# Layer 1 attention of a two-layer cross-attention kernel: probabilities turned by DMA transposes instead of TensorE transposes

## The reference, cut to what matters

```
Q = (X @ Wq.T + bq).reshape(b, 56, 16, 64)
KV = (encoder_out @ Wkv.T + bkv).reshape(b, 1500, 16, 128)
K, V = (KV[..., :64], KV[..., 64:])
scores = einsum('bqhd,bkhd->bhqk', Q, K) / 8
weights = softmax(scores, axis=-1)
attn = einsum('bhqk,bkhd->bqhd', weights, V).reshape(b, 56, 1024)
out = attn @ Wo.T + bo
```

## Time and profile before

| what | value |
|---|---|
| median of 3 runs | 1374.76 us |
| the profiled execution's own time | 1373.72 us |
| its span in the trace | 1372.0 us |
| mean granted TensorE clock | 0.973 |
| TensorE busy | 1226.6 us, 89% of the span |
| VectorE busy | 1025.5 us, 75% |
| ScalarE busy | 769.0 us, 56% |
| GpSimd busy | 395.4 us, 29% |

### The profile page before, as it was taken

The page is one execution under the profiler, slowest core; times in us unless marked ns, Lnnn a source line. Parts: engine busy times, 40 slices in busy tenths (PEclk is TensorE's granted clock), DMA queues, the critical chain, the costliest instruction groups (busy, mean ns, idle before and its releaser), DMA issues.

```text
span 1372.0 us, 27813 instructions
## 1 busy us (share of the span) xinstructions
PE 1226.6 (89%) x10406; PEld 772.9 (56%) x10408; DVE 1025.5 (75%) x1661; ACT 769.0 (56%) x1013; POOL 395.4 (29%) x248
## 2 busy tenths in 40 slices
PE   0868999999999997888799999999999999999974
PEld 0335566666666566334456666656666666666642
DVE  6657666666666646877788888888888888888877
ACT  0534455555555455455666666666666666666642
POOL 5357665666666414332000000000000000000000
PEclk9989999999999997999999999999999999999996
DMA  5333344344234420010011110011110011110000
GB/s 150 78 79 86 85 106 108 80 112 110 79 97 108 113 61 7 0 46 0 3 43 46 46 39 25 27 45 45 45 44 19 27 45 45 45 44 24 1 0 14
DMA packets 29717, 74.66 MB, mean 54 GB/s; under 512 B 6384, under 2 KB 14960, under 8 KB 29664
## 3 DMA queue, kind: packets, MB, share of 16 engines
q1 hardware_dynamic: 23408, 70.78, 17.6%
q10 hardware_dynamic: 6256, 3.16, 0.9%
HBM read 42.30 MB, written 0.46 MB: 31 GB/s over the span
## 4 chain that ended last, share of the span: by engine, by line
PE 69%; DVE 13%; issue 8%; ACT 6%; ACTq 3%; DVEq 0%; POOL 0%
PE bank L825 13%; PE bank L807 13%; PE bank L767 8%; PE bank L683 7%; PE bank L707 5%; PE bank L711 5%; PE bank L724 4%; DVE bank_max L1495 3%; ACTq L415 2%; DVE region L1636 2%; ACT region L1139 2%; PE bank L796 2%; PE bank L848 2%; PE bank L785 2%; DVE e_row L1456 2%
## 5 line engine op out<-in xcount | busy, mean ns | idle before, releaser
L1456 DVE CUSTOM_DVE_ANT_0 e_row<-bank,region 112x1500 f32<-112x1500 f32 x128 | 220.2, 1720 | 128.9 <-PE bank L683 128.8
L1174 ACT CAST region<-bank 125x768 f16<-125x768 f32 x224 | 178.7, 798 | 207.9 <-PE bank L767 207.9
L1139 ACT ACTIVATE region<-bank 125x896 f32<-125x896 f32 x192 | 176.0, 917 | 210.4 <-PE bank L711 210.4
L807 PE MATMUL bank<-region 128*128 128x500 f16 x1008 | 236.1, 380 | 14.7 <-ACT e_row L1165 13.3
L1514 DVE TENSOR_TENSOR region<-bank,region 125x768 f16<-125x768 f32 x224 | 209.6, 953 | 25.7 <-ACT region L1174 25.7
L1495 DVE TENSOR_REDUCE bank_max<-bank 128x1 f32<-128x500 f32 x336 | 208.9, 671 | 11.9 <-PE bank L807 11.9
L513 POOL TENSOR_TENSOR region<-c_in,region 125x1536 f16<-125x1536 f32 x16 | 49.7, 3108 | 562.2 <-ACT region L1189 562.2
L767 PEld LDWEIGHTS bank<-ident,e_row 128*125 128x125 f32 x1344 | 175.9, 188 | 31.3 <-DVE region L1514 5.5
L767 PE MATMUL bank<-ident,e_row 128*125 128x128 f32 x1344 | 179.6, 274 | 3.3 <-DVE region L1514 2.6
L1165 ACT ACTIVATE e_row<-bank,neg_max 128x1500 f32<-128x1500 f32 x112 | 169.7, 1515 | 20.1 <-DVE neg_max L1499 19.9
L807 PEld LDWEIGHTS bank<-region 128*128 (+1 forms) x1008 | 93.7, 98 | 116.4 <-issue 12.8
(11 more groups left out here) (211 smaller groups left out, 1483.4 us busy)
## 6 DMA issues: line engine op xcount, KB each, us to landing
c_in<-in_ctx SPq DMA_DIRECT2D x32, 750.0 KB
region<-region SPq DMA_DIRECT2D x64, 192.0 KB, 2.7
region<-in_mask_Bx1xSxS_if SPq DMA_DIRECT2D x32, 328.1 KB
region<-region SPq DMA_DIRECT2D x64, 96.0 KB, 2.5
region<-region SPq DMA_DIRECT2D x8, 750.0 KB
g_w<-region SPq DMA_DIRECT2D x8, 750.0 KB
g_w<-in_L_ffn_rt_gate ACTq DMA_DIRECT2D x1, 1024.0 KB, 9.8
u_w<-in_L_ffn_rt_up ACTq DMA_DIRECT2D x1, 1024.0 KB, 17.8
```

Source lines behind the costliest of these rows:

```text
L807: last = pe.matmul(bank[:, k, 0:4 * KP], q1[:, ql, b, 128 * t:128 * (t + 1)], c_t1[par][:, cl, 4 * k:4 * k + 4, 0:KP], start=(ql == 0 and ...
L1139: act.activation(p0[:, 2 * i:2 * i + 2, :], ring0("s", h, i)[0:KP, :, 0:HALF_ROWS], ACT.Exp, scale=SCALE0)\
L1174: act.copy(p_high1[grp][:, UC * u:UC * (u + 1), 128 * at:128 * (at + 1)], pair_chunks(unit_no(1, par, ("turn", t, u)), 128)).then_inc(sem( ...
L1456: dve.tensor_tensor_reduce(out=masked.rearrange("p (a k) -> p a k", a=3), in0=bank[0:R0, 0:3, 0:4 * KP], in1=mask_bias[par][:].rearrange(" ...
```

## The change

Layer 1's loop is written anew.

- The scores have two sets of three banks, 0 to 2 and 3 to 5, in turn (`score_banks1`), and one semaphore step for each tile. Scores of tile n wait for the exponential of tile n-2.
- One VectorE instruction takes the maximum of 1500 columns in place of four.
- `e_row` is not scaled any more. VectorE scales the row's sum and takes its reciprocal (`dve_inv1`); ScalarE writes the high half straight from `e_row` with that factor (`act_high1`, one instruction of 1500 columns), VectorE the low half (`dve_low1`, one instruction of 1500). Both go to `halves1`, two buffers of 128 x 2 halves x 12 chunks x 128 columns (padded from 125), which lie in memory that holds weights earlier.
- One DMA transpose for each tile, on SyncE's queue, turns both halves into `p1` (`sync_turn1`): 24 blocks of 128x128 float16, 786,432 bytes. The high half of tile n waits until tile n-2 has been turned, since they share a buffer.
- The context's halves are turned by such a DMA as well (`sync_turn_context1`), issued behind tile 1's; TensorE's `pe_prep` and ScalarE's copies remain for batch 0 alone.
- SyncE's queue has in every batch: the load of the next context, the turns of tiles 0 and 1, the context's turn, tiles 2 to 4, the copy to `c_keep1`, tiles 5 and 6. The engine waits before each for what it needs, in this order.
- The products move back: group 0's three parts come after tile 6's scores slot and in the next batch's slots 0 and 1; group 1's in its slots 3 to 5. Each group has a bank of its own, 6 and 7.

The diff's core, with what the prediction speaks of:

```diff
+        U_BANK1 = (6, 7)
+        def score_banks1(par, t):
+            first = 3 * ((t + par) % 2)
+            return bank[:, first:first + 3, 0:4 * KP]
...
+        def turned1(b, par, t):
+            return sem(f"turned1_{(t + par) % 2}"), 56 * (b - par) + 16 * ((T1 * par + t) // 2 + 1)
+        def sync_turn1(sp, b, par, t):
+            grp = 0 if t < GROUPS1[1][0] else 1
+            first = GROUPS1[grp][0]
+            if t == first:
+                wait_apart(sp, "sp", (sem("pv_done1"), 2 * (b - 1) + grp + 1))
+            wait_apart(sp, "sp", (sem("low_done1"), b * T1 + t + 1))
+            sp.dma_start_transpose(p1[grp][:, :, :, 128 * (t - first):128 * (t - first + 1)].rearrange("p n c r -> p (n c) r"),
+                                   halves1[(t + par) % 2].rearrange("p n c k -> p (n c k)"))\
+                .then_inc(turned1(b, par, t)[0], 16)
+        def sync_turn_context1(sp, b, par):
+            wait_apart(sp, "sp", (sem("split_done1"), b + 1))
+            wait_apart(sp, "sp", (sem("scores1"), (b - 1) * T1))
+            sp.dma_start_transpose(c_t1[par].rearrange("p n c k -> p (n c) k"), c_split1.rearrange("p n c e -> p (n c e)"))\
+                .then_inc(sem("c_turned1"), 16)
...
             def layer1(b, par, first, last):
                 if not last:
                     sync_load_context(sp, 1, b + 1, 1 - par)
-                    sync_keep(sp, b + 1, 1 - par)
+                for t in range(T1):
+                    sync_turn1(sp, b, par, t)
+                    if t == 1 and not last:
+                        sync_turn_context1(sp, b + 1, 1 - par)
+                    if t == GROUPS1[1][0] and not last:
+                        sync_keep(sp, b + 1, 1 - par)
...
         def pe_scores1(pe, b, par, t):
...
-            wait(pe, sem("exp_done1"), b * T1 + t)
+            wait(pe, sem("exp_done1"), b * T1 + t - 1)
...
         def pe_pv1(pe, b, par, grp, first, end):
...
-                pe.wait_ge(sem("low_done1"), b * (2 * T1) + 2 * z)
-                wait(pe, sem("u_done1"), b * 2 + grp)
+                for t in (z - 2, z - 1):
+                    pe.wait_ge(*turned1(b, par, t))
+                wait(pe, sem("u_done1"), 2 * b + grp - 1)
...
-                    pe_turn(pe, 1, b, par, t, (0,))
-                    if t == 0:
-                        pe_turn(pe, 1, b, par, t, (1,))
-                    if t < 3 and not first:
-                        pe_pv1(pe, b - 1, 1 - par, 1, 4 * t, 4 * t + 4)
-                    if t >= 4:
-                        pe_pv1(pe, b, par, 0, 4 * (t - 4), 4 * (t - 3))
+                    if t < 2 and not first:
+                        pe_pv1(pe, b - 1, 1 - par, 0, 4 * (t + 1), 4 * (t + 2))
+                    if 3 <= t < 6 and not first:
+                        pe_pv1(pe, b - 1, 1 - par, 1, 4 * (t - 3), 4 * (t - 2))
+                    if t == 6:
+                        pe_pv1(pe, b, par, 0, 0, 4)
+                    if t == 6 and par == 0 and not first:
                         pe_proj1(pe, b)
...
         def act_exp1(act, b, par, t):
             act.wait_ge(sem("max_done1"), b * T1 + t + 1)
-            wait(act, sem("turned1"), (b * T1 + t - 1) * 2)
+            wait(act, sem("low_done1"), b * T1 + t - 1)
...
+        def act_high1(act, b, par, t):
+            act.wait_ge(sem("inv_done1"), 2 * (b * T1 + t) + 2)
+            if not (isinstance(b, int) and b == 0 and t < 2):
+                ready, count = turned1(b, par, t)
+                act.wait_ge(ready, count - 16)
+            act.activation(halves1[(t + par) % 2][:, 0, :, 0:KP], e_row[(t + par) % 2][:].rearrange("p (c k) -> p c k", c=KC),
+                           ACT.Copy, scale=row_inv[:, t:t + 1]).then_inc(sem("high_done1"), 1)
...
         def act_split1(act, b, par):
             act.wait_ge(sem(f"ctx_in1_{par}"), per_use(b, par, 16))
-            wait(act, sem("ct_turned1"), 2 * b)
-            wait(act, sem("kept1"), 16 * b)
-            act.copy(c_split1[0:KP, :, 0, :], c_in[par][:]).then_inc(sem("high1"), 1)
+            if not (isinstance(b, int) and b == 0):
+                act.wait_ge(sem("ct_turned1"), 2)
+                wait(act, sem("c_turned1"), 16 * (b - 1))
+                act.wait_ge(sem("kept1"), 16 * b)
+            act.copy(c_split1[0:KP, 0], c_in[par][:]).then_inc(sem("high1"), 1)
...
                     if t == 1 and not last:
                         act_split1(act, b + 1, 1 - par)
...
+                    act_high1(act, b, par, t)
                     if t < T1 - 1:
                         act_exp1(act, b, par, t + 1)
                     elif not last:
                         act_exp1(act, b + 1, 1 - par, 0)
...
         def dve_max1(dve, b, par, t):
-            for k in range(3):
-                dve.wait_ge(sem("scores1"), (b * T1 + t) * 3 + k + 1)
-                dve.tensor_reduce(bank_max[:, t, k:k + 1], bank[:, k, 0:4 * KP], AX.X, ALU.max, negate=True)\
-                    .then_inc(sem("bank_max"), 1)
...
+            dve.tensor_reduce(neg_max[:, t:t + 1], score_banks1(par, t), AX.XY, ALU.max, negate=True)\
+                .then_inc(sem("max_done1"), 1)
...
+        def dve_low1(dve, b, par, t):
+            dve.wait_ge(sem("high_done1"), b * T1 + t + 1)
+            half = halves1[(t + par) % 2]
+            dve.scalar_tensor_tensor(half[:, 1, :, 0:KP], e_row[(t + par) % 2][:].rearrange("p (c k) -> p c k", c=KC),
+                                     row_inv[:, t:t + 1], half[:, 0, :, 0:KP], ALU.mult, ALU.subtract)\
+                .then_inc(sem("low_done1"), 1)
...
             def layer1(b, par, first, last):
                 for t in range(T1):
                     nxt = (b, par, t + 1) if t < T1 - 1 else (b + 1, 1 - par, 0)
+                    dve_inv1(dve, b, par, t)
+                    if not (last and t == T1 - 1):
+                        dve_max1(dve, *nxt)
+                    dve_low1(dve, b, par, t)
...
```

204 lines of the change are left out of this document (61 added, 143 removed).

## The result

The kernel after takes 1506.95 us (median of 4, 1505.90 to 1507.38), the kernel before beside it 1374.74 (median of 4). The ratio is 1.0968, 95% interval 1.0943 to 1.0993: slower by 132 us. I had forecast slower, by 41. The time lies in the range and the sign is right; the size is off by a factor of three. The profiled execution took 1506.82 us, span 1505.1, mean granted clock 0.883 (before: 0.973).

The account below looks back on a forecast made before the run. The prediction took SyncE's queue of turns, copy and load to bound the changed loop at 44.3 us a batch, 3.2 more than now. 14 x 3.2 - 7 + 3 = +41 us on 1373.7 gave 1415, range 1285 to 1570.

Parts of the forecast that it names:

- D: Time for which one turn of 786,432 bytes holds the DMA engines, taken as 3.2 us, near the 16-engine copies' row.
- step 1: After the context's load lands: ScalarE's split 1.48, tile 1's high half 1.45 and low half 1.72, together 4.7 us.
- the formula: One batch's loop through SyncE's queue and ScalarE, four steps plus 0.5 for semaphores: 25.1 + 6D, 44.3 us.
- Both ends that I leaned on, 1.8 and 3.4: Estimates of a turn's time: 1.8 us from five engines' rate scaled to sixteen, 3.4 from 16-engine copies within the chip.
- rival C: Turns dearer than copies, 6.2 us each from 24 blocks going one by one; some 1670 us; chance 0.16.
- C's sign: What would show C: landings over 8 us with DMA engines busy throughout, or SyncE held for microseconds by an issue.
- step 2: Issue and landing 1.85 us plus three turns in line (tile 1's, the context's, tile 2's): 1.85 + 3D.
- step 3: Tile 4's high and low half, after tile 2's turn frees their buffer: 3.2 us.
- step 4: Tile 4's turn, the copy, turns of 5 and 6, the next load, before the next split: 14.85 + 3D.
- -7 + 3: Ends: batches 0 and 15 at 37.5 us each, -7 in all; last exponential to last copy-out about 18 us, +3.
- A: Turns as fast as five engines' ports suggest, D about 2.1: 1329 us, 1357 at worst with halved clock; chance 0.27.
- B: Queue does not hold turns behind the 5-engine transfers; 36 us a batch, 1298 us; chance 0.14.

Follow-up runs that it names:

- e1: Kernel after, with the context's copy moving 128 rows and the load cut in 112 and 13 rows: 1403.82 us, ratio 1.0208.
- e4: Kernel after, with only the high halves turned, 12 blocks a tile instead of 24 (output not the reference's): 1351.73 us, ratio 0.9834.
- e7: Kernel after, each tile's turn replaced by a plain copy of 128 pieces of 6144 bytes, nothing turned: 1391.92 us, ratio 1.0126.
- e5: Kernel after, copy and loads issued from ScalarE's queue, still on 5 engines, the load a batch earlier: 1417.06 us, ratio 1.0305.
- e3: Kernel after, each tile's turn replaced by a plain copy of the same 3072 pieces of 256 bytes, unturned: 1510.16 us, ratio 1.0986.
- e10: Kernel after, with GpSimd's subtraction waiting for tile 1's low half: 1481.46 us, ratio 1.0776.
- e9: Kernel after, copy and loads on ScalarE's queue and spread over 16 engines, loads a batch earlier, context's turn behind tile 1's: 1373.35 us, ratio 0.9990.
- e12: On e11, each tile turned by two DMAs, one per half, the high half's sent as soon as it is written: 1304.65 us, ratio 0.9492.
- e13: Kernel after with only the edit of two turns of 12 blocks a tile, copy and load unchanged: 1435.90 us, ratio 1.0447.
- e11: e9 and e10 together, against the kernel before: 1373.14 us, ratio 0.9985.

## Why the prediction was right and wrong

**That a line of transfers decides, and makes the kernel slower: right.** TensorE busy 68% and waiting for exponentials, ScalarE waiting for the load and for the turns of the buffers, all as forecast. e1 shows the five engines' part, e4 and e7 that the price of a turn is the other part. The sentence that the order of SyncE's queue is what holds a turn was too narrow: e5 took the two transfers out of that queue and the turns still took 7.6 to 10.3 us.

**"I take 3.2: near the 16-engine row": this step failed.** D is 3.9: 3.6 of transfer at 217 GB/s and 0.3 until the next. 6 x 0.7 = 4.2 us a batch, 59 of the missing 91 us; step 1 below is 22, and what is left, about 10, is the formula's own error (0.4 a batch), the batch before (41.0 and not 41.1) and the ends. Both ends that I leaned on, 1.8 and 3.4, came from copies in longer pieces. The lower one is what e7 shows for pieces of 6144 bytes, 430 GB/s. The rate of the earlier trace rows, which I followed, came out close to the turn's by luck: those copies move 3072 bytes in each of their 64 rows, and nothing in them said what pieces of 256 bytes cost (what held them at 215 to 234 GB/s no run shows). The price of 256-byte pieces was in no row, and I gave them 0.16 as rival C, which put it far too high at 6.2. C's sign came half true: the issue does hold SyncE. But e3 shows that this by itself costs nothing here: with copies of the same rate that are issued in 0.63 the kernel takes the same time.

**Step 1, 4.7 us: measured 6.3.** The high half is 1.55, and the low half beside GpSimd's subtraction 3.27. I named the subtraction as running beside and costed it at nothing. e10 prices this: 1.6 a batch, 25 us in all. This is a second step that failed, an overlap taken as free.

**Steps 2 to 4.** In the batch above, step 2 from 1091.02 to 1104.61 is 13.6 us (forecast with D = 3.9: 13.55); step 3 3.5 (3.2); step 4 from 1108.07 to the next split at 1134.90 26.8 (26.55). So the formula held for the kernel after: 25.1 + 6 x 3.9 + 1.6 = 50.1, measured 50.5 in the mean and 50.2 in this batch. On other kernels it is rougher. For e4, whose trace has half turns issued 1.7 us apart where nothing holds them (1051.86, then 1053.58), it gives 25.1 + 5 x 1.7 + 3.9 + 1.6 = 39.1, measured 40.3. For e7, with 1.8 for each of the five long copies and 3.9 for the context's turn, it gives 39.6, measured 42.9; it comes closer, 42.4, only if a copy is counted as its landing less the forecast's overhead, 4.2 - 1.85 = 2.35.

**Batch 0, batch 15 and the end.** Forecast -7 + 3. The loop alone makes +133 of +132 us, so both together are about -1. The end, in the timeline of the kernel after:

```profile
1453.29 0.19 ACT L1132 ACTIVATION_READ_ACCUMULATOR e_row<-bank,neg_max 128x1 f32 x1
...
1465.61 6.01 PE L798 MATMUL bank<-region,g_w 125*128 125x384 f16 x36
...
1471.66 0.49 ACT L1148 ACTIVATE region<-bank 128x384 f32<-128x384 f32 x1 [4.44 <-PE bank L798]
```

From the last read-out to the last copy-out are 18.4 us (forecast 18, before 15). The +3 holds, and the -7 was too much by some 3.

**Rivals.** A and B fall: in the kernel after no turn lands under 5.4 us, and no turn behind the copy lands before it has freed the engines. The clock that I priced only in A is real here as well, since TensorE idles 8.9 us before tile 2's scores and runs them at 0.50, 1.85 us longer. No run isolates what this costs in all; in the batch above the next wait, for a turn, mostly covers it.

**What I did not price: the two buffers.** The formula has them in it as waits for a landing, and therefore came out right for this order. But it took them for a part of the queue's line. e9 has gaps in which the DMA engines move nothing, and is not faster than before; e12, with turns by halves, fills these gaps. In the kernel as changed it is worth 4.4 us a batch (e13), on e11 4.9.
